# Attention stage of an audio tower on one Trainium2 core: row maxima turned on VectorE instead of TensorE, and a new order of dense products, copies, reciprocals and page clears

## The chip, the cores and the metric

The kernel runs on one core of a Trainium2 chip. The metric is the device time of one execution in microseconds, the median of several runs. The core has TensorE (PE in the rows, with PEld for its weight loads), VectorE (DVE), ScalarE (ACT), GpSimd (POOL) and SyncE (SP), whose queue issues most DMAs. Each engine works through its own list of instructions in order and waits on semaphores.

## What is computed

The input is 32 sequences of 375 tokens and 256 features. A causal mix over 32 taps with two dense layers gives `h` (376 tokens). Then come attention and a mixture-of-experts layer, each with a layer norm ahead of it and a residual behind it. Only the attention is touched by the change:

```python
q = (x @ wq + bq).reshape(b, s, h, hd).transpose(0, 2, 1, 3)      # 16 heads of 16
k = (x @ wk + bk).reshape(b, s, h, hd).transpose(0, 2, 1, 3)
v = (x @ wv + bv).reshape(b, s, h, hd).transpose(0, 2, 1, 3)
scores = jnp.einsum('bhqd,bhkd->bhqk', q, k) / jnp.sqrt(jnp.float32(hd))
scores = jnp.where(causal, scores, -jnp.inf)
weights = jax.nn.softmax(scores, axis=-1)
attn = jnp.einsum('bhqk,bhkd->bhqd', weights, v)
...
return attn @ wo + bo
```

## The kernel before

The attention phase is a software pipeline over the 32 sequences. One **step** `b` works on several sequences at once: the token mix of sequence b+3 (`mix`), layer norm, queries and keys of b+2 (`front`), the values and row maxima of b+1 (`maxima`), the exponentials of b (`attend`) and the output product of b-1 (`finish`). Steps run from -3 to 32; those from 1 to 28, twenty-eight in all, hold every part. Two steps stand in a hardware loop.

A step has 28 **units** on every engine, `n = 7*g + u` with four groups `g` (half of the heads is `g // 2`) of seven units `u`. In each unit TensorE computes scores twice: once with queries as rows for `neg_max` (L584, masked by the bf16 product of L601), which VectorE reduces to the negated row maximum (L830, function `maxima`), and once with keys as rows (L618), which ScalarE turns into exponentials (L739, `exps`). The first form has three PSUM banks, so unit n needs the maxima of unit n-3 (unit 27 and the first ones of a step have their own rule); the second has two, so unit n needs the exponentials of unit n-2. GpSimd masks the exponentials (L949) and TensorE multiplies them with the values (L654) behind units 4, 11, 18 and 25. ScalarE copies these products out (`keep`), GpSimd adds the parts of a half (`join`), VectorE shuffles the sums and takes reciprocals in four quarters (`gather_sums`: piece 0 is the shuffle L884, pieces 1 to 4 are L890), and GpSimd scales the result and splits it (`normalise`).

Between units TensorE does the **dense** products, which share two banks in turn: `hid` (n = 1, 2), `val` (7, 27), `nT` (transposes of the normed rows, L540, 9 and 10), `q` (13, 15), `k` (16, 18), `out` (21, 23), `conv` (24, 25), and `maxT` (5, 20). A product may start when the one before the last has been read. Most are read twice, since a value is carried as a high and a low float32r part: ScalarE writes the high part (`take_hi`), VectorE the low one (`take_lo`).

The maximum must be subtracted inside the exponential's product. So q_rows holds, beside three times 16 rows of queries per 64-row half of the array, two more rows, the high and low part of the negated maximum, against rows of ones in k_rows. `neg_max` has queries on partitions, so `max_T` turns it on TensorE (L566, three transposes per half), `take_hi` and `take_lo` split it (L705, L815), and four DMAs of SyncE (`max_rows`, L1088) lay it into q_rows. Half 0 is turned at unit 20 and needed at unit 0 of the next step, half 1 at unit 5 and needed at unit 14 (`open_exp` waits for max_loaded). Before a new sequence's maxima are computed these rows are set to zero by two DMAs per half (L1072).

SyncE's queue in a step, in order: the maxima of half 1 (4 DMAs), queries and keys of half 0 (`rows`, L1064: 6 each, and the 2 zero DMAs), the maxima of half 0 (4), the store of the finished rows (2, after `out1` is read), the next input (2, after `conv1` is computed), queries and keys of half 1 (14, after the step's last exponentials). That is 40 DMAs. ScalarE's queue clears two pages of DRAM of 816 KB each (L746) after units 9 and 11.

## Time and profile before

| | |
|---|---|
| time, median of 3 runs | 2151.53 us (2150.16 to 2156.01) |
| the profiled execution's own time | 2163.89 us |
| its span, first to last instruction | 2162.1 us |
| attention phase | to about 1309 us of the span |
| one full step of it | 36.95 us |
| busy in one full step | PE 35.82, DVE 30.43, ACT 22.99, POOL 19.55 us |

The routing phase and the expert pages follow the attention phase and are the same code before and after. Within a full step TensorE has almost no idle time; the number to watch is the step's length, times the count of steps.

### The profile page before, as it was taken

The page shows a single profiled execution, that of the slowest core. Times are in us where ns is not written, and L with a number is a line of the kernel's source. Part 1 is how long each engine was busy: PE and PEld are TensorE (multiplying, and loading weights), DVE is VectorE, ACT ScalarE, POOL GpSimd, SP SyncE. Part 2 cuts the span into 40 slices and gives each one's busy share as a digit, 9 for nine tenths or more (in the row PEclk, how much of TensorE's full clock was granted, in tenths as well). Part 3 has the DMA queues.
Part 4 walks back from the last instruction along what each step waited for, and adds up shares of the span by engine and source line. Part 5 has one row for each costly group of instructions (what it writes and reads, how often), then busy time and mean ns, then how long its engine had stood idle before and what let it go on. Part 6 is the DMA issues. An engine that isn't in the chain of part 4 may idle for free. (4 is left out here: it accounts for less than half of the span.)

```text
span 2162.1 us, 49812 instructions
## 1 busy us (share of the span) xinstructions
PE 1836.0 (85%) x14801; PEld 1434.1 (66%) x14802; DVE 1416.7 (66%) x3857; ACT 988.2 (46%) x2112; POOL 1054.0 (49%) x1443
## 2 busy tenths in 40 slices
PE   4899999999999999999999875877787749768674
PEld 4777777777777777777777644666666638757663
DVE  3468888888788888888887735656566542434343
ACT  1156566666566666656665543322223204323231
POOL 3035555455555555555555553445555431455555
PEclk7579999999999999999999976888888879889996
DMA  2334434434343434343433412222222246778785
GB/s 74 68 98 137 129 134 132 136 126 144 115 149 117 133 131 131 132 130 134 131 133 114 137 62 91 81 72 88 88 89 83 89 111 223 245 241 267 249 259 183
DMA packets 214515, 291.09 MB, mean 135 GB/s; under 512 B 44854, under 2 KB 176666, under 8 KB 214426
## 3 DMA queue, kind: packets, MB, share of 16 engines
q1 hardware_dynamic: 178010, 186.11, 28.2%
q0 software_dynamic: 18048, 49.31, 7.4%
q10 hardware_dynamic: 18368, 54.64, 6.6%
q8 instruction: 38, 0.62, 0.1%
q14 instruction: 51, 0.42, 0.1%
HBM read 83.25 MB, written 129.69 MB: 98 GB/s over the span
## 5 line engine op out<-in xcount | busy, mean ns | idle before, releaser
L830 DVE TENSOR_REDUCE neg_max<-bank 120x1 f32<-120x376 f32 (+2 forms) x896 | 523.6, 596 | 231.8 <-PE bank L584 228.0
L739 ACT ACTIVATE probs<-bank 128x376 f32<-128x376 f32 (+2 forms) x896 | 446.8, 520 | 270.3 <-PE bank L618 265.9
L584 PE MATMUL bank<-k_rows,q_rows 64*128 64x128 f32 (+2 forms) x1536 | 420.7, 354 | 5.4 <-DMA q_rows<-maxT_lo 4.6
L618 PE MATMUL bank<-q_rows,k_rows 64*120 64x120 f32 (+2 forms) x1536 | 382.4, 341 | 2.9 <-ACT probs L739 2.8
L949 POOL TENSOR_SCALAR_AFFINE_SELECT probs<-probs 128x512 f32<-128x512 f32 (+1 forms) x384 | 233.0, 625 | 232.3 <-ACT probs L739 232.3
L601 PE MATMUL bank<-causal,own_row 56*120 56x56 bf16 (+4 forms) x1792 | 310.5, 253 | 14.3 <-DMA k_rows<-k_flat_hi 8.2
L1815 POOL DMA_INDIRECT x_sorted<-r_normed,route x188 | 183.2, 974 | 202.2 <-DVE route L1662 149.8
L2171 POOL DMA_INDIRECT y_got<-y_sorted,p_route x188 | 182.5, 971 | 192.2 <-issue 185.2
L584 PEld LDWEIGHTS bank<-k_rows,q_rows 64*128 64x128 f32 (+1 forms) x1536 | 254.8, 192 | 8.6 <-DMA q_rows<-maxT_lo 5.5
L618 PEld LDWEIGHTS bank<-q_rows,k_rows 64*128 64x128 f32 (+1 forms) x1536 | 234.6, 186 | 8.0 <-ACT probs L739 5.1
L601 PEld LDWEIGHTS bank<-causal,own_row 64*128 64x128 bf16 (+2 forms) x1792 | 152.6, 117 | 129.6 <-issue 60.0
L654 PE MATMUL bank<-probs,val 128*32 128x376 f32 (+2 forms) x3072 | 194.3, 387 | 2.6 <-POOL probs L949 2.6
L890 DVE RECIPROCAL recip<-sums 128x94 f32<-128x94 f32 x256 | 185.1, 726 | 0.1
L654 PEld LDWEIGHTS bank<-probs,val 128*32 128x32 f32 (+1 forms) x3072 | 89.0, 112 | 98.3 <-issue 78.4
L975 POOL TENSOR_TENSOR attn_raw<-attn_raw,recip 128x376 f32<-128x376 f32 x64 | 63.6, 994 | 140.0 <-DVE recip L890 140.0
L2010 PE MATMUL pbank<-w_gate_up,xT 128*128 x816 | 114.5, 298 | 15.7 <-issue 14.9
L2010 PEld LDWEIGHTS pbank<-w_gate_up,xT 128*128 128x128 f32 x816 | 106.8, 210 | 19.6 <-issue 19.3
L2102 DVE SCALAR_TENSOR_TENSOR p_gated<-p_tanh,pbank 128x256 f32<-128x256 f32 x51 | 21.4, 420 | 145.3 <-ACT p_tanh L2064 114.5
L1500 DVE SCALAR_TENSOR_TENSOR r_tanh<-r_tanh,rbank 128x512 f32<-128x512 f32 (+1 forms) x48 | 32.2, 671 | 122.7 <-ACT r_tanh L1435 113.8
L1332 PE MATMUL rbank<-r_normedT_hi,r_up_hi 128*128 128x512 f32 (+1 forms) x96 | 49.3, 514 | 73.3 <-DVE r_hidden L1509 70.9
L1364 PE MATMUL rbank<-shared_down,r_hidden 128*128 128x256 f32 x376 | 99.1, 409 | 12.1 <-DVE base L1518 6.8
L1002 POOL TENSOR_TENSOR resid<-hid,bias_o 128x256 f32<-128x256 f32 (+1 forms) x96 | 67.6, 732 | 72.0 <-DVE out_rows L874 72.0
(226 smaller groups left out, 4294.6 us busy)
## 6 DMA issues: line engine op xcount, KB each, us to landing
x_sorted<-zeros ACTq DMA_DIRECT2D x32, 816.0 KB, 4.1
y_sorted<-zeros ACTq DMA_DIRECT2D x32, 816.0 KB, 4.3
x_rows<-x_sorted SPq DMA_DIRECT2D x51, 512.0 KB
y_sorted<-p_y_rows SPq DMA_DIRECT2D x51, 512.0 KB
q_rows<-q_flat_hi SPq DMA_DIRECT2D x256, 94.0 KB
k_rows<-k_flat_hi SPq DMA_DIRECT2D x248, 94.0 KB
q_rows<-q_flat_lo SPq DMA_DIRECT2D x128, 94.0 KB
out_dram<-base SPq DMA_DIRECT2D x47, 256.0 KB
```

What stands on the lines that cost most here:

```text
L584: last = eng.matmul(ps[0:T[t], m * w:(m + 1) * w], q[rows, slot, t * P:t * P + T[t]], k[rows, slot, 0:w], start=False, stop=(m == len(head ...
L601: eng.matmul(dst, own_row[group, h, 0:d], causal[group, h, 0:m, first:d], start=(h == 1), stop=False, skip_group_check=True)
L618: last = eng.matmul(ps[0:T[t], m * w:(m + 1) * w], k[64 * c:64 * c + 64, slot, t * P:t * P + T[t]], q[64 * c:64 * c + 64, slot, t * P:S], ...
L654: last = eng.matmul(bank_pv[32 * j:32 * j + 32, t * P:S], val[par][0:kk, t, 4 * (g // 2) + j, 32 * e:32 * e + 32], probs[g % 2][0:kk, j, O ...
L739: eng.activation(probs[g % 2][0:T[t], first:first + len(heads), OFF[t]:OFF[t] + w], bank_exp[n % 2][0:T[t], 0:len(heads) * w].rearrange("k ...
L830: eng.tensor_reduce(dst, src, AX.X, ALU.max, negate=True).then_inc(max_taken, 1)
L890: eng.reciprocal(recip[:, cols], sums[:, cols]).then_inc(recip_done, 1)
L949: eng.affine_select(out=blk, in_=blk, compare_op=ALU.is_ge, fill=0.0, base=0, pattern=[[0, 4], [1, d]], channel_multiplier=-1).then_inc(pr ...
L1364: last = eng.matmul(bank_y[t // 2][:, t % 2 * D:(t % 2 + 1) * D], hidden[c][:, t * P:(t + 1) * P], experts.down[:, c, :], start=(c == 0 an ...
L1815: eng.indirect_dma_start(x_sorted, at, normed[st.b % 4][:, t, :], None)\
L2010: last = eng.matmul(bank_gu[par][:, a * 2 * MR:(a + 1) * 2 * MR], xT[par][a // 2][:, k, a % 2 * P:(a % 2 + 1) * P], routed.gate_up[:, k, e ...
L2171: eng.indirect_dma_start(y_got[ring][:, t, k, :], None, y_sorted, at)\
```

## The change

The maxima are no longer turned on TensorE. VectorE copies the high part of `neg_max` and the low part into a tile of 32 columns per token tile, transposes all 32x32 blocks of it at once (`turn_maxima`, before unit 19 for half 0 and after unit 4 for half 1), and four DMAs lay it into q_rows, in pieces of 32 values (128 bytes). For this the four rows for the maxima of both array halves are made neighbours (rows 62 to 65), and q_rows is padded to 384 columns. The zeros take one DMA per half instead of two. A step now has 14 dense products instead of 16, and their places change: both `nT` behind unit 9, both `k` behind unit 17, `out` at 20 and 22, `conv` at 24 and 27, where `val1` follows. ScalarE keeps the value products one unit earlier (11, 18, 25), clears the pages after units 14 and 16, and makes `k` and `conv` copies at the new places. VectorE does both `hid` sums and the norm's statistics after unit 2, each low part one unit earlier where it can, and the reciprocals at other units. GpSimd joins half 0 a group earlier and adds the residual a group later.

```diff
-    ROWS = 3 * sh.HD
+    ROWS = (0, P - 3 * sh.HD)
+    MAX_ROW = P // 2 - 2
+    SPAN = NT * P
...
-        q_rows = [sb(f"q_rows{p}", [P, 8, S], F32R) for p in range(2)]
+        q_rows = [sb(f"q_rows{p}", [P, 8, SPAN], F32R) for p in range(2)]
...
-        maxT = [sb(f"maxT_{s}", [8, 2, S], F32R) for s in ("hi", "lo")]
+        max_parts = [sb(f"max_parts{h}", [P, NT, 32], F32R) for h in range(2)]
+        max_turned = [sb(f"max_turned{h}", [P, NT, 32], F32R) for h in range(2)]
...
-                return (["hid0", "hid1"] * front + ["maxT1"] * attend + ["val0"] * maxima
-                        + ["nT0", "nT1", "q0", "q1", "k0", "k1"] * front + ["maxT0"] * maxima
+                return (["hid0", "hid1"] * front + ["val0"] * maxima
+                        + ["nT0", "nT1", "q0", "q1", "k0", "k1"] * front
                         + ["out0", "out1"] * finish + ["conv0", "conv1"] * mix + ["val1"] * maxima)
...
-                def max_T(st, half, shift):
-                    ps = open_bank(st, f"maxT{half}")
-                    eng.wait_ge(max_taken, st.at(shift, GROUPS * UNITS, 2 * UNITS * (half + 1)))
-                    for t in range(NT):
-                        last = eng.transpose(ps[0:8, t * P:t * P + T[t]], neg_max[0:T[t], t, half, :],
-                                             ident[0:T[t], 0:T[t]])
-                    close(last)
...
-                        if n == 5 and st.attend:
-                            max_T(st, 1, 0)
                         if n == 7 and st.maxima:
                             values(st, 0)
-                        if n in (9, 10) and st.front:
-                            normed_T(st, n - 9)
+                        if n == 9 and st.front:
+                            normed_T(st, 0)
+                            normed_T(st, 1)
                         if n in (13, 15) and st.front:
                             query_key(st, "q", (13, 15).index(n), w_q)
-                        if n in (16, 18) and st.front:
-                            query_key(st, "k", (16, 18).index(n), w_k)
-                        if n == 20 and st.maxima:
-                            max_T(st, 0, 1)
-                        if n in (21, 23) and st.finish:
-                            out_rows_(st, (21, 23).index(n))
-                        if n in (24, 25) and st.mix:
-                            conv(st, n - 24)
+                        if n == 17 and st.front:
+                            query_key(st, "k", 0, w_k)
+                            query_key(st, "k", 1, w_k)
+                        if n in (20, 22) and st.finish:
+                            out_rows_(st, (20, 22).index(n))
+                        if n in (24, 27) and st.mix:
+                            conv(st, (24, 27).index(n))
                         if n == 27 and st.maxima:
                             values(st, 1)
...
-                        if n == 9 and st.attend:
+                        if n == 14 and st.attend:
                             clear_pages(st, x_sorted)
-                        if n == 11 and st.attend:
+                        if n == 16 and st.attend:
                             clear_pages(st, y_sorted)
-                        if n == 5 and st.attend:
-                            take_hi(st, "maxT1", maxT[0][0:8, 1, :], 8)
                         if n == 5 and st.finish:
                             keep(st, 3, -1)
                         if n == 7 and st.front:
                             normalise(st)
                         if st.front and n in (9, 10):
                             take_hi(st, f"nT{n - 9}", nT[st.b % 2][0][:, n - 9, :])
+                        if n in (11, 18) and st.attend:
+                            keep(st, (11, 18).index(n), 0)
                         if st.front and n == 13:
                             if not (isinstance(st.i, int) and st.b == -2):
                                 for h in range(2):
-                                    eng.wait_ge(rows_loaded[(st.b + 1) % 2][h], st.turn(1, 224, 224))
+                                    eng.wait_ge(rows_loaded[(st.b + 1) % 2][h], st.turn(1, 208, 208))
                         if st.front and n in (13, 15):
                             j = (13, 15).index(n)
                             take_hi(st, f"q{j}", q_flat[0][:, j, :], bias=bias_q[:, j:j + 1])
-                        if n in (12, 19, 26) and st.attend:
-                            keep(st, (12, 19, 26).index(n), 0)
-                        if st.front and n in (16, 18):
-                            j = (16, 18).index(n)
-                            take_hi(st, f"k{j}", k_flat[0][:, j, :], bias=bias_k[:, j:j + 1])
-                        if n == 20 and st.maxima:
-                            take_hi(st, "maxT0", maxT[0][0:8, 0, :], 8)
-                        if st.mix and n in (24, 25):
-                            take_hi(st, f"conv{n - 24}", mixed[0][:, n - 24, :])
+                        if st.front and n == 17:
+                            for j in range(2):
+                                take_hi(st, f"k{j}", k_flat[0][:, j, :], bias=bias_k[:, j:j + 1])
+                        if st.mix and n in (25, 27):
+                            j = (25, 27).index(n)
+                            take_hi(st, f"conv{j}", mixed[0][:, j, :])
+                        if n == 25 and st.attend:
+                            keep(st, 2, 0)
...
-                HALF_1_AT, HALF_0_AT = (10, 11, 12, 13, 16), (22, 24, 25, 26, 27)
-                HI = ["maxT1", "nT0", "nT1", "q0", "q1", "k0", "k1", "maxT0", "conv0", "conv1"]
+                HALF_1_AT = {10: (0, 1), 12: (2,), 14: (3,), 16: (4,)}
+                HALF_0_AT = {21: (0,), 23: (1, 2), 25: (3,), 26: (4,)}
+                HI = ["nT0", "nT1", "q0", "q1", "k0", "k1", "conv0", "conv1"]
...
+                def turn_maxima(st, half, shift):
+                    parts = max_parts[half][:, :, 0:16].rearrange("q t (c s m) -> q t c s m", c=2, s=2)
+                    whole = neg_max[:, :, half, :].rearrange("q t (c m) -> q t c m", c=2)
+                    done = st.at(shift, 2, half + 1)
+                    eng.wait_ge(max_taken, st.at(shift, GROUPS * UNITS, 2 * UNITS * (half + 1)))
+                    eng.tensor_copy(parts[:, :, :, 0, :], whole).then_inc(max_hi, 1)
+                    eng.wait_ge(max_hi, done)
+                    eng.tensor_tensor(parts[:, :, :, 1, :], whole, parts[:, :, :, 0, :].bitcast(F32), ALU.subtract)\
+                        .then_inc(max_lo, 1)
+                    eng.wait_ge(max_lo, done)
+                    eng.transpose(max_turned[half][:, :, :].rearrange("q t i -> q (t i)").bitcast(F32),
+                                  max_parts[half][:, :, :].rearrange("q t i -> q (t i)").bitcast(F32)).then_inc(max_turns, 1)
...
+                        if st.finish and n == 25:
+                            out_sum(st, 1)
+                        if st.mix and n == 26:
+                            take_lo(st, "conv0", mixed[1][:, 0, :], mixed[0][:, 0, :])
+                        if n == 19 and st.maxima:
+                            turn_maxima(st, 0, 1)
+                        if st.finish and n == 21:
+                            out_sum(st, 0)
                         if st.maxima:
                             maxima(st, g, u)
-                        if st.front and n in (2, 3):
-                            hid_out(st, n - 2)
-                            if n == 3:
-                                norm_stats(st)
-                        if n == 6 and st.attend:
-                            take_lo(st, "maxT1", maxT[1][0:8, 1, :], maxT[0][0:8, 1, :], 8)
+                        if st.front and n == 2:
+                            hid_out(st, 0)
+                            hid_out(st, 1)
+                            norm_stats(st)
+                        if n == 4 and st.attend:
+                            turn_maxima(st, 1, 0)
+                        if st.maxima and n == 7:
+                            values(st, 0)
+                        if st.front and n in (9, 10):
+                            j = n - 9
+                            take_lo(st, f"nT{j}", nT[st.b % 2][1][:, j, :], nT[st.b % 2][0][:, j, :])
                         if st.finish and n in HALF_1_AT:
-                            gather_sums(st, 1, -1, HALF_1_AT.index(n))
-                        if st.maxima and n in (8, 27):
-                            values(st, (8, 27).index(n))
-                        if st.front and n in (10, 11):
-                            j = n - 10
-                            take_lo(st, f"nT{j}", nT[st.b % 2][1][:, j, :], nT[st.b % 2][0][:, j, :])
-                        if st.front and n in (14, 16):
-                            j = (14, 16).index(n)
+                            for piece in HALF_1_AT[n]:
+                                gather_sums(st, 1, -1, piece)
+                        if st.front and n in (13, 15):
+                            j = (13, 15).index(n)
                             take_lo(st, f"q{j}", q_flat[1][:, j, :], q_flat[0][:, j, :], bias=bias_q[:, j:j + 1])
-                        if st.front and n in (17, 19):
-                            j = (17, 19).index(n)
-                            take_lo(st, f"k{j}", k_flat[1][:, j, :], k_flat[0][:, j, :], bias=bias_k[:, j:j + 1])
-                        if n == 21 and st.maxima:
-                            take_lo(st, "maxT0", maxT[1][0:8, 0, :], maxT[0][0:8, 0, :], 8)
+                        if st.front and n == 17:
+                            for j in range(2):
+                                take_lo(st, f"k{j}", k_flat[1][:, j, :], k_flat[0][:, j, :], bias=bias_k[:, j:j + 1])
                         if st.attend and n in HALF_0_AT:
-                            gather_sums(st, 0, 0, HALF_0_AT.index(n))
-                        if st.finish and n in (22, 23):
-                            out_sum(st, n - 22)
-                        if st.mix and n in (25, 26):
-                            j = n - 25
-                            take_lo(st, f"conv{j}", mixed[1][:, j, :], mixed[0][:, j, :])
+                            for piece in HALF_0_AT[n]:
+                                gather_sums(st, 0, 0, piece)
+                        if st.mix and n == 27:
+                            take_lo(st, "conv1", mixed[1][:, 1, :], mixed[0][:, 1, :])
+                        if st.maxima and n == 27:
+                            values(st, 1)
...
-                        if g == 2 and st.attend:
+                        if g == 1 and st.attend:
                             join(st, 0, 0)
-                        if g == 2 and st.maxima:
+                        if g == 3 and st.maxima:
                             residual(st)
...
-                        for c in range(2):
-                            at, slots = 64 * c + ROWS, slice(4 * half, 4 * half + 4)
-                            eng.dma_start(q_rows[par][at:at + 2, slots, :].bitcast(F32),
-                                          q_rows[par][at + 2:at + 4, slots, :].bitcast(F32)
-                                          ).then_inc(rows_loaded[par][half], 16)
+                        at, slots = MAX_ROW, slice(4 * half, 4 * half + 4)
+                        eng.dma_start(q_rows[par][at:at + 4, slots, 0:S].bitcast(F32),
+                                      q_rows[par][at + 4:at + 8, slots, 0:S].bitcast(F32)
+                                      ).then_inc(rows_loaded[par][half], 16)
...
-                    _, k = st.product(f"maxT{half}")
-                    eng.wait_ge(dense_read, k + 1)
-                    for c in range(2):
-                        for part in range(2):
-                            row_ = 64 * c + ROWS + part
-                            eng.dma_start(q_rows[par][row_:row_ + 1, 4 * half:4 * half + 4, :].bitcast(F32),
-                                          maxT[part][4 * c:4 * c + 4, half, :].bitcast(F32)).then_inc(max_loaded[par][half], 16)
+                    wait_alone(eng, max_turns, st.at(shift, 2, half + 1), passed_sp)
+                    rows_ = q_rows[par][MAX_ROW:MAX_ROW + 4, 4 * half:4 * half + 4, :].bitcast(F32)\
+                        .rearrange("r m (t b i) -> r m t b i", b=4, i=32)
+                    for b in range(4):
+                        eng.dma_start(rows_[:, :, :, b, :], max_turned[half][32 * b:32 * b + 16, :, :].bitcast(F32)
+                                      ).then_inc(max_loaded[par][half], 16)
```

## Rows read from the trace of the kernel before

**Rows 1.** The page: busy time, and the granted clock in 40 slices

```profile
PE 1836.0 (85%) x14801; PEld 1434.1 (66%) x14802; DVE 1416.7 (66%) x3857; ACT 988.2 (46%) x2112; POOL 1054.0 (49%) x1443
...
PE   4899999999999999999999875877787749768674
...
PEclk7579999999999999999999976888888879889996
```

**Rows 2.** Busy time by stretch: one full step

```profile
602.55:639.50 36.95, 35.82 (x352) 26.73 (x352) 30.43 (x66) 22.99 (x49) 19.55 (x29) 1.00 0.39 131
```

**Rows 3.** Waits, 200 to 1200 us: total, times, longest

```profile
PE bank L515 <- DVE out_rows L874: 14.0, 27, 0.6
PE bank L494 <- DVE normedT_lo L815: 12.8, 27, 0.5
...
PEld bank L584 <- DMA q_rows<-maxT_lo: 1.1, 1, 1.1
```

**Rows 4.** Timeline of TensorE in one step: start, duration, line

```profile
602.08 0.23 PE L601 MATMUL bank<-causal,own_row 56*120 56x56 bf16 x1
...
602.55 0.49 PE L566 MATMUL bank<-ident,neg_max 128*8 128x128 f32 x3
602.97 0.23 PE L601 MATMUL bank<-causal,own_row 56*120 56x56 bf16 x1
...
612.70 0.28 PE L601 MATMUL bank<-causal,own_row 64*128 64x256 bf16 x1
...
620.31 0.23 PE L601 MATMUL bank<-causal,own_row 56*120 56x56 bf16 x1
...
620.59 0.33 PE L618 MATMUL bank<-q_rows,k_rows 64*128 64x376 f32 x1
...
632.34 0.28 PE L601 MATMUL bank<-causal,own_row 64*128 64x256 bf16 x1
```

**Rows 5.** Timeline of VectorE in the same step

```profile
600.47 0.55 DVE L830 TENSOR_REDUCE neg_max<-bank 120x1 f32<-120x376 f32 x1
600.93 0.41 DVE L839 TENSOR_TENSOR hid<-bank,bias_mix 120x256 f32<-120x256 f32 x1
...
602.71 1.46 DVE L830 TENSOR_REDUCE neg_max<-bank 120x1 f32<-120x376 f32 x3
```

**Rows 6.** Groups by form, 200 to 1200 us: busy, mean ns

```profile
L884 DVE STREAM_SHUFFLE sums<-sums_swapped 128x376 f32<-128x376 f32 x54 | 31.7, 587 | 0.5
...
L815 DVE TENSOR_TENSOR maxT_lo<-bank,maxT_hi 8x376 fp32r<-8x376 f32 x54 | 28.7, 531 | 0.0
...
L705 ACT ACTIVATE maxT_hi<-bank 8x376 fp32r<-8x376 f32 x54 | 25.1, 465 | 0.0
```

**Rows 7.** Groups by form on VectorE behind the attention phase

```profile
L1577 DVE TENSOR_TENSOR beyond<-rbank,spare 128x16 f32<-128x16 f32 x24 | 4.1, 171 | 32.3 <-PE rbank L1378 20.8 <-issue 7.9 <-remote 3.5
...
L1537 DVE CAST top_nof<-top_no 128x8 f32<-128x8 uint32 x23 | 3.7, 163 | 0.1
```

**Rows 8.** Timeline of SyncE's queue in the same step: issue start, duration

```profile
607.73 0.63 SPq L1088 DMA_DIRECT2D q_rows<-maxT_lo  x1
617.72 1.29 SPq L1064 DMA_DIRECT2D q_rows<-q_flat_hi  x2
...
629.06 0.57 SPq L1088 DMA_DIRECT2D q_rows<-maxT_lo  x1
```

**Rows 9.** DMA issues of the whole run: count, size, us to landing

```profile
probs<-in_L_tok_bv_dram SPq DMA_DIRECT2D x2, 0.5 KB, 2.3
page_dram<-page_expert SPq DMA_DIRECT2D x2, 0.5 KB, 6.5
```

**Rows 10.** DMA packets from 606 to 613 us

```profile
DMA packets 636, 1.76 MB, mean 252 GB/s; under 512 B 64, under 2 KB 124, under 8 KB 636
```

**Rows 11.** Late attention phase: SyncE issue, TensorE wait, the clock behind it

```profile
1235.47 1.39 SPq L1088 DMA_DIRECT2D q_rows<-maxT_lo  x1
...
1239.35 0.47 PE L584 MATMUL bank<-k_rows,q_rows 64*128 64x128 f32 x1 [3.11 <-DMA q_rows<-maxT_lo]
...
1240.00:1242.00 2.00, 2.00 (x22) 1.90 (x20) 1.38 (x2) 1.15 (x2) 0.00 (x0) 0.50 0.00 0
```

16 lines of the change are left out of this document (11 added, 5 removed).

## The prediction, made before the changed kernel was run

> **What bounds the kernel now.** I read the page first. TensorE is busy in 85% of the span, and its slices stand at 9 through the first 22 of 40, which is the attention phase, with the clock granted in full from the fifth slice on [rows 1]. Then I cut one full step out by its repeating products: 36.95 us long, TensorE busy 35.82, VectorE 30.43, ScalarE 22.99 and GpSimd 19.55 [rows 2]. So within a step TensorE is the bound, and whatever shortens its list by a microsecond shortens the step by one, as long as nobody makes it wait instead. The waits confirm it and show what is left. TensorE stops at two places once per step: before q0, for the low part of `nT1`, 12.8 us in 27 steps, and before conv0, for VectorE's read of `out0`, 14.0 us in 27 [rows 3]. These are 0.47 and 0.52 us per step. DMA waits for the maxima came once in that stretch [rows 3]. The phase holds 28 full steps; the four or five ragged ones at each end wait for other things. The rest of the program is untouched.
>
> **TensorE's list.** From the timeline of one step [rows 4]:
>
> - A turn of the maxima takes from 602.55 to 602.97, 0.42 us. Two per step go: 0.84.
> - A unit with dense work behind it takes 0.47 (602.08 to 602.55), one with another unit right behind it 0.28 (620.31 to 620.59). Each interruption between units thus costs 0.19 beside its own work. There are 18 interrupted places in a step before (1, 2, 4, 5, 7, 9, 10, 11, 13, 15, 16, 18, 20, 21, 23, 24, 25, 27) and 15 after, since 5, 10 and one of 20/21 go and the other moves cancel. 3 x 0.19 = 0.57. From below I take nothing for it (the gap may come back at another seam), from above 0.57; I take 0.57, because the two spacings are of the same kind of unit.
>
> **The two stalls.** Both transposes now come behind unit 9, and VectorE takes the low parts at 9 and 10 ahead of the shuffle and the reciprocal, where they stood behind them. q0 still comes behind unit 13, so its 0.47 goes. `out0` is now multiplied behind unit 20 and read before unit 21's maximum, while before it was read behind unit 22's maximum and a shuffle; conv0 stays at 24. Its 0.52 goes too. Together 0.99.
>
> **A new stall.** VectorE does both `hid` sums and the statistics behind unit 2, so the maximum of unit 3 comes after them; before it stood between the sums. The second sum and the statistics take from 600.93 to 602.71, 1.78 us [rows 5]. They would begin at 600.47 and end at 602.25, and unit 3's maximum would end 0.46 later (1.46 for three running on), at 602.7. Unit 6 uses the same bank. Without the turn it could start at 602.08 + 0.28 = 602.36 [rows 4]. TensorE waits 0.35 there, and some 0.05 for the semaphore: 0.4. What is late next is unit 7 by 0.1 at most, then the 12 products of val0 give VectorE time to catch up. From below 0, from above 0.9 if the sum waits for its product too.
>
> **VectorE.** It loses two low parts of 0.531 us [rows 6], 1.06 per step. It gains twice a copy, a difference and a block transpose, in line, each waiting for the one before. The first two are small: 0.163 and 0.171 for shapes nearest to them [rows 7]. No transpose of blocks is in the trace. The nearest row is the shuffle within 32 partitions, 0.587 for 376 columns [rows 6]; 96 columns cannot cost more, and not less than a smallest instruction, 0.16. I take 0.25. That is 2 x 0.58 = 1.2 against 1.06. VectorE stays at 30.5 us in a step of 35, 87% busy, and the turns stand where it is ahead of TensorE by more than that (val0 behind unit 7, out0 behind unit 20). I cost them at nothing; without that cover they cost 1.2. The Trainium skill, in "VectorE: DVE Perf Modes", section "The three transpose paths", gives 311 ns for a 128x128 bf16 block transpose on VectorE, and no run shows one yet. By it VectorE's addition would be 1.3 us and the step the same.
>
> **The pairs and the other engines.** k0 and k1 in a row keep VectorE from unit 18's maximum until both low parts are done, and ScalarE from its exponential. TensorE can run three units ahead by the maxima and two by the exponentials, and behind unit 18 it has a value product, behind unit 20 `out0`. I find no wait, but such places are tight: conv1 must be read before `hid0` behind unit 1, GpSimd's residual now ends about when VectorE wants it, the join stands ahead of three masks that unit 25 needs. I bound this from 0 to 1.0 per step and take 0.3, since the present schedule shows stalls of 0.5 at just such places. ScalarE loses 2 x 0.465 [rows 6]; it is idle for a third of the step, so nothing.
>
> **The queue of SyncE.** 38 DMAs instead of 40, at some 0.65 us of issue each. For half 0 the last one was issued at 629.63 (629.06 + 0.57, rows 8) and unit 0 of the next step came at 632.34 [rows 4]: 2.7 us to land, which was enough but for one case in 27 [rows 3]. Afterwards the chain starts with q1's low part at least one maximum (0.55) earlier, has one zero DMA less (0.65), and TensorE arrives 0.42 + 0.19 + 0.52 = 1.1 earlier: 2.8 us. For half 1 the last issue ended at 608.36 [rows 8] and unit 14 came at 612.70 [rows 4], 4.3 us. It gains 0.65, TensorE comes 0.9 sooner, and the chain may start up to 1.0 later because `load_x` now waits for conv1 behind unit 27: 3.1 us. The pieces change: now 48 per DMA of 128 bytes, 192 in all. The four DMAs before were cut into pieces below 512 bytes as well, 64 packets of them in the window that holds the four [rows 10], so this is three times as many, spread over 16 engines at 40% load. I take no cost. The clears come three to five units later, off half 1's maxima and onto the first rows of the next half.
>
> **The sum.** Per full step: 0.84 + 0.57 + 0.99 - 0.4 - 0.3 = 1.70. 28 x 1.70 = 48. The eight other turns of the ragged steps give 8 x 0.6 = 5. In one ragged step TensorE stood 3.11 us for the maxima of half 1, whose issues were stretched to 1.39 us by the clears, and ran at the lower clock for some microseconds after it [rows 11]. With the clears later and one DMA less I take 2 off. In all 55 of the profiled execution's own time of 2163.89 (its span is 2162.1). Its median neighbours were 2151.53, so the forecast is 2151.53 x (1 - 55/2163.89) = 2097.
>
> **The rivals.**
>
> - **Main: as summed**, 2.3 at best and 1.2 at worst per full step: 28 x 2.3 + 10 = 74 to 28 x 1.2 + 3 = 37, that is 2078 to 2115.
> - **VectorE becomes the pace.** It had 36.95 - 30.43 = 6.5 us of waits per step [rows 2], each one for a unit not yet computed. If it can lose only a sixth of them because its new bursts (hid and statistics, two k, two reciprocals at 23) make TensorE wait in turn, the step is 30.5 + 5.4 = 35.9, a gain of 1.05, 30 us: 2122. For it speaks the busy share of 87%; against it that TensorE waits for maxima nowhere now.
> - **The maxima land late.** This is the one that ends slower. If the DMAs of 128-byte pieces need as long as the one of many tiny pieces did, 6.5 us, and not 2.3 as its neighbour [rows 9], unit 0 waits 6.5 - 2.8 = 3.7 and unit 14 waits 3.4. Per step 7.1 - 1.7 = 5.4 more, 28 x 5.4 = 151: 2302, and more if the clock falls as in rows 11. It decides from a landing time of about 3.9 us, where both waits together (3.9 - 2.8 and 3.9 - 3.1) eat 1.9. The Trainium skill, "DMA: Bandwidth & Descriptors", section "Specifications", says that below 512 bytes a transfer does not reach line rate because the engine reads, modifies and writes. It speaks against this change, and the present pieces are below that bound already.
> - **No change**: the gains are eaten by waits at the tight places, 1.7 or so per step; 2145 to 2158.
>
> **Chances.** Main 0.76, VectorE's pace 0.13, late maxima 0.06, no change 0.05. 0.3%, about 6 us, is about what a measurement of this kernel can tell from no change. Faster by more than that: 0.76 + 0.13 and the small part of late maxima that still gains, 0.90. Same 0.05, slower 0.05. The range takes in the main case and VectorE's pace with some room: 2074 to 2128.
>
> **What would show it.** After: a full step of about 35.2 us; no instruction on neg_max by TensorE; TensorE's waits before q0 and conv0 gone; a wait of about 0.4 at unit 6 for VectorE's maximum; VectorE's block transposes at 0.2 to 0.3 us; the new DMAs' issue still at 0.6 us, and no wait of scores for the turned maxima in full steps; the 3.11 wait in the ragged step about halved. The prediction is wrong if waits for `neg_max` or `probs` appear at several units of each step, if the new DMAs take clearly longer to issue or to land, or if the interruptions keep their price when there are fewer.

## The result, and the profile after

The changed kernel takes 2057.12 us (median of 4 runs, 2053.22 to 2071.27) against 2150.85 for the kernel before on the same chip (4 runs, 2143.12 to 2156.01): a ratio of 0.9587, 95% interval 0.9543 to 0.9630. The forecast was 2097 with a range from 2074 to 2128. The direction was right. The gain was 94 us where 54 were forecast, and the time is outside the range.

The page of the changed kernel, as in [rows 1]: TensorE has 67 us less to do and its share of the span stays at 85%.

```profile
PE 1768.9 (85%) x14609; PEld 1413.7 (68%) x14610; DVE 1436.8 (69%) x3985; ACT 968.6 (47%) x2048; POOL 1052.4 (51%) x1446
...
PE   4799999999999999999999848777787759667774
...
PEclk8589999999999999999999858888898879898897
```

One full step, cut at the same product as in [rows 2]; the columns are length, PE, PEld, DVE, ACT, POOL, the granted clock, the share of the DMA engines, GB/s:

```profile
589.55:623.59 34.04, 33.92 (x345) 26.23 (x346) 31.00 (x69) 22.32 (x47) 19.55 (x30) 1.00 0.57 141
```

It is 2.91 us shorter. TensorE was idle for 1.13 us of a step and now is for 0.12; the other 1.9 us is work and spacing that went, and short waits of the weight loads, which the row counts as busy. VectorE has 31.00 us of 34.04, 91%.

The measure for the comparisons below is the mean full step: the time from the start of the norm statistics in step 1 to that in step 29, divided by 28. It was 36.96 us (158.42 to 1193.23) and is 34.08 (147.83 to 1102.04). By the same landmarks the phase shrank by 98.4 us: 28 x 2.88 = 80.6 in the full steps, 10.6 ahead of them and 7.2 behind them. The program behind the phase took 5.8 us longer in the profile after (858.9 against 853.1), so that the profiled executions differ by 92.6 us. The stretch ahead of the full steps is not the change's alone: its length was 147.8, 141.6 and 152.1 us in three profiles of the same changed kernel and 136.3 to 148.2 us in ten variants of it, and it holds the time at the lower clock. The third of these profiles, at 152.1, is of an execution that was 1.5% slower than the fastest of its kernel.

The waits of TensorE from 200 to 1100 us (total, times, longest), to be held against [rows 3]:

```profile
PEld bank L602 <- DVE neg_max L829: 31.0, 129, 0.4
...
PE bank L585 <- DMA q_rows<-max_turned: 0.3, 1, 0.3
```

The waits for `normedT_lo` and `out_rows` are not in the list any more. What stands there is the weight load that waits for VectorE's maxima, in 129 short pieces. Its longest piece is in the timeline of TensorE at unit 6, which is the second row here; the third is unit 7:

```profile
592.54 0.13 PEld L602 LDWEIGHTS bank<-causal,own_row 56*120 56x120 bf16 x1 [0.19 <-issue]
...
593.20 0.13 PEld L602 LDWEIGHTS bank<-causal,own_row 56*120 56x120 bf16 x1 [0.37 <-DVE neg_max L829]
...
593.66 0.11 PEld L602 LDWEIGHTS bank<-causal,own_row 64*128 64x128 bf16 x2 [0.17 <-DVE neg_max L829]
```

VectorE in the same stretch, the turn in three instructions:

```profile
592.60 1.01 DVE L829 TENSOR_REDUCE neg_max<-bank 120x1 f32<-120x376 f32 x2
...
593.52 0.17 DVE L837 CAST max_parts<-neg_max 128x24 fp32r<-128x24 f32 x1
...
593.72 0.18 DVE L839 TENSOR_TENSOR max_parts<-neg_max,max_parts 128x24 fp32r<-128x24 f32 x1
```

And the instructions on `max_turned` in the whole run (count, shortest, median and longest ns), the DMAs' issue and the block transpose:

```profile
L1104 SPq DMA_DIRECT2D q_rows<-max_turned x256: 639/652/822, 96.2 to 1165.6; - x128
L842 DVE STREAM_TRANSPOSE max_turned<-max_parts x64: 277/278/279, 93.0 to 1163.1; 128x96 f32<-128x96 f32 x64
```

So the small prices of the forecast hold. The block transpose takes 278 ns (taken: 0.25 us), the copy and the difference 0.17 and 0.18, the issue of a DMA 0.652. The maxima land in time but for 0.3 us in one step.

### The profile page after: what moved, and what is told of

It is laid out like the page before. It is cut to its first block and busy times, and to the rows that moved or that the text cites. A ratio compares the mean times of both kernels' runs of the same rounds, so it can differ in the third digit from the quotient of the medians.

```text
span 2069.5 us, 49314 instructions
## 1 busy us (share of the span) xinstructions
PE 1768.9 (85%) x14609; PEld 1413.7 (68%) x14610; DVE 1436.8 (69%) x3985; ACT 968.6 (47%) x2048; POOL 1052.4 (51%) x1446
## 2 busy tenths in 40 slices
DMA packets 226547, 291.12 MB, mean 141 GB/s; under 512 B 57142, under 2 KB 188954, under 8 KB 226458
## 3 DMA queue, kind: packets, MB, share of 16 engines
q1 hardware_dynamic: 190042, 186.14, 36.3%
## 5 line engine op out<-in xcount | busy, mean ns | idle before, releaser
L738 ACT ACTIVATE probs<-bank 128x376 f32<-128x376 f32 (+2 forms) x896 | 440.7, 529 | 279.7 <-PE bank L619 267.9
L829 DVE TENSOR_REDUCE neg_max<-bank 120x1 f32<-120x376 f32 (+2 forms) x896 | 508.0, 587 | 60.4 <-PE bank L585 55.8
L585 PE MATMUL bank<-k_rows,q_rows 64*128 64x128 f32 (+2 forms) x1536 | 411.6, 350 | 4.0 <-ACT probs L738 2.5
L619 PE MATMUL bank<-q_rows,k_rows 64*120 64x120 f32 (+2 forms) x1536 | 373.0, 338 | 3.3 <-ACT probs L738 3.1
L602 PE MATMUL bank<-causal,own_row 56*120 56x56 bf16 (+4 forms) x1792 | 305.4, 250 | 18.3 <-DMA k_rows<-k_flat_hi 11.7
L2136 DVE COPY p_y_rows<-pbank 128x512 f32<-128x512 f32 x51 | 35.2, 689 | 90.4 <-remote 59.7
```

The source lines that it names most:

```text
L585: last = eng.matmul(ps[0:T[t], m * w:(m + 1) * w], q[rows, slot, t * P:t * P + T[t]], k[rows, slot, 0:w], start=False, stop=(m == len(head ...
L602: eng.matmul(dst, own_row[group, h, 0:d], causal[group, h, 0:m, first:d], start=(h == 1), stop=False, skip_group_check=True)
L619: last = eng.matmul(ps[0:T[t], m * w:(m + 1) * w], k[64 * c:64 * c + 64, slot, t * P:t * P + T[t]], q[64 * c:64 * c + 64, slot, t * P:S], ...
L738: eng.activation(probs[g % 2][0:T[t], first:first + len(heads), OFF[t]:OFF[t] + w], bank_exp[n % 2][0:T[t], 0:len(heads) * w].rearrange("k ...
L829: eng.tensor_reduce(dst, src, AX.X, ALU.max, negate=True).then_inc(max_taken, 1)
```

## The experiments

Ten variants ran, and the changed kernel twice more, on four chips. `e1` to `e4` ran on the first, `e5`, `e7`, `e8` and `after_again` on the second, `e9`, `e10` and `after_timed` on the third, and `e11` on the fourth. The kernel before took 2162.62, 2160.3 and 2181.02 us on the first, third and fourth. On the second it took 1993.3; the changed kernel's full step there was 34.06 us and its attention phase ended at 1207.3 us against 1210.6, so that the difference between the chips lies behind the phase. So steps are compared between chips, and times only on one. Ratios are to the kernel before on the same chip; where none is given, the kernel ran once. Diffs are against the changed kernel and are cut; the places of the copies and reads move along with them.

### The two halves of the change, each alone

`e1_turn_only`: the kernel before with the new turn; TensorE's products at their old places.

```diff
-                        if n == 9 and st.front:
-                            normed_T(st, 0)
-                            normed_T(st, 1)
+                        if n in (9, 10) and st.front:
+                            normed_T(st, n - 9)
...
-                        if n == 17 and st.front:
+                        if n in (16, 18) and st.front:
...
-                        if n in (20, 22) and st.finish:
+                        if n in (21, 23) and st.finish:
...
-                        if n in (24, 27) and st.mix:
+                        if n in (24, 25) and st.mix:
```

> The kernel before with the new way to turn alone (VectorE turns, 128-byte DMA pieces, rows 62 to 65), all other work in its old order. Theory A (each part of a full step has its own price and the prices add): two turns of 0.42 us and two interruptions of 0.19 go, the waits before q0 and conv0 stay, so a full step is 36.95 - 1.2 = 35.7 us and the run about 2151 - 28 x 1.2 - 5 = 2112 us, ratio 0.982. Theory B (VectorE's list is the pace at the tight places and the turn gains only with the new order): the added instructions of VectorE lengthen the waits for it, step 36.2 or more, ratio 0.99 or more. The share of the DMA engines rises from 0.40 to nearly 0.6 in a full step under both, since the pieces are the same as in the changed kernel.

Measured: 2158.95 us, ratio 0.9991 (0.9951 to 1.0031), full step 37.03 us. Theory A fails and theory B holds: the turn alone gives nothing. TensorE has two products less and waits instead:

```profile
PEld bank L525 <- DVE out_rows L881: 27.9, 25, 1.1
PE bank L525 <- DVE out_rows L881: 21.6, 25, 0.9
...
PE bank L504 <- DVE normedT_lo L808: 12.5, 24, 0.6
...
PE bank L602 <- DVE neg_max L823: 8.6, 24, 0.4
...
PE bank L585 <- ACT probs L736: 4.7, 25, 0.2
```

The wait ahead of conv0 grew from 0.52 to 0.86 us (21.6 in 25), the one ahead of q0 is 0.52 (0.47 before), and two come in that did not exist: 0.36 per step for the maxima, at unit 6, and 0.19 for ScalarE's exponentials, at unit 21. The DMA engines' share was expected at nearly 0.6 and is 0.45; the last section comes back to it.

`e2_order_only`: the changed kernel with the turn given back to TensorE; all else in the new order.

```diff
+                        if n == 5 and st.attend:
+                            max_T(st, 1, 0)
...
+                        if n == 20 and st.maxima:
+                            max_T(st, 0, 1)
```

> The changed kernel's order with the old way to turn (TensorE at units 5 and 20, ScalarE and VectorE parts, four row DMAs). Theory A with a cover: in the changed kernel TensorE waits 0.37 us at unit 6 for the maximum of unit 3; here a turn of 0.42 stands just there and hides that wait, so a step is 34.04 + 0.84 + 0.19 - 0.4 = 34.7 us, and the run about 2151 - 28 x 2.25 - 10 = 2078, ratio 0.966. Plain additivity instead (no cover): 34.04 + 1.22 = 35.3, ratio 0.974. The 10 us that the changed kernel gains before the first full step (its clock returns sooner) are gained here if they come from the order, and not if they come from the turn. DMA share stays at 0.40.

Measured: 2080.34 us, ratio 0.9618 (0.9583 to 0.9653), full step 34.53 us. The order alone gives 2.43 us per full step. The turn on top of it gives 34.53 - 34.08 = 0.45. The theory with a cover is near (34.7 expected), plain additivity (35.3) is not. The DMA engines' share did not stay at 0.40; it is 0.50. The stretch ahead of the full steps is 144.1 us here and 148.2 in `e1`, against 158.4 before, so it shrank with either half and decides nothing between them.

From TensorE's timelines, the stretches of a full step in us, start to start, each the mean of 27 steps ("turn" is `maxT`; all other stretches agree within 0.04 us):

```
stretch                          before   e1     e2     after
units 5 to 7, turn                2.05    2.05   2.00   1.93
units 8, 9                        1.06    0.98   1.12   0.92
nT and the units between/behind   1.90    1.97   1.59   1.60
units 12, 13                      1.35    1.41   0.81   0.80
k pair, units, value product      5.16    5.16   4.96   4.94
units 19 to 24, turn, out         6.55    6.56   5.61   5.40
conv1, unit 26/27, val1           2.66    2.66   2.47   2.47
units 0, 1                        1.48    1.50   1.25   1.25
```

### The order taken back piece by piece

`e7_nT_late`: VectorE takes the transposes' low parts one unit later, behind the shuffle.

```diff
-                HALF_1_AT = {10: (0, 1), 12: (2,), 14: (3,), 16: (4,)}
+                HALF_1_AT = {10: (0,), 11: (1,), 12: (2,), 13: (3,), 16: (4,)}
...
-                        if st.front and n in (9, 10):
+                        if st.front and n in (10, 11):
```

> The changed kernel with the low parts of nT at units 10 and 11 behind the shuffle and the reciprocal again (reciprocals at 10, 11, 12, 13, 16). My step: the wait before q0 comes back, about 0.5 us, a full step of 34.5 to 34.6. Rival: the pair of transposes already brought q0 its input in time, 34.1.

Measured: 34.70 us per full step, 1909.34 us. Against 34.06 on the same chip the step lost 0.64, 0.1 more than expected, and the wait ahead of q0 is back. In one step's timeline:

```profile
217.11 0.44 PE L504 MATMUL bank<-normedT_hi,w_q_hi 128*128 128x376 f32 x1 [0.56 <-DVE normedT_lo L814]
```

`e11_out_late`: the last product's halves back at units 21 and 23. VectorE's shuffle of half 0 moves from 21 to 22, and its read of `out0` goes behind unit 22's maximum. The expectation misnames two things: the halves stand at units 20 and 22 in the changed kernel, and the wait of 0.52 is the one ahead of conv0, not of the queries' product.

```diff
-                        if n in (20, 22) and st.finish:
-                            out_rows_(st, (20, 22).index(n))
+                        if n in (21, 23) and st.finish:
+                            out_rows_(st, (21, 23).index(n))
```

> The changed kernel with the two halves of the last product put back from units 19 and 22 to units 21 and 23, as before; the rest as changed. Theory (the early halves give the chain behind them, rescale and y_out, its time, and save 0.5 us per full step at the wait ahead of the first half of the queries' projection): the wait of about 0.52 us in front of that projection returns, and the full step is 34.6 to 34.8 us instead of 34.08. Rival (ScalarE and GpSimd now stand at other units, and the chain is in time anyway; what was saved in this stretch is only seams): 34.05 to 34.25 us. Single run, to be read by the full step: mean of the 27 full steps from sequence 1 to sequence 28.

Measured: 34.98 us per full step, 2116.09 us. Neither theory nor rival held: 0.90 us lost, more than the stall it was to bring back. The waits from 200 to 1100 us:

```profile
PEld bank L585 <- ACT probs L738: 25.7, 26, 1.0
...
PE bank L585 <- ACT probs L738: 16.8, 26, 0.7
...
PE bank L525 <- DVE out_rows L887: 4.3, 26, 0.3
```

Ahead of conv0 the product's own wait is 0.17 per step, not 0.52. The larger part is 0.65 at unit 21, where TensorE stands for ScalarE. In its timeline, two copies of a value product lie ahead of the exponential:

```profile
620.13 0.57 ACT L723 ACTIVATE sum_of_even<-bank,strip_half 128x376 f32<-128x376 f32 x1 [0.91 <-PE bank L655]
...
620.60 0.57 ACT L724 ACTIVATE attn_of_even<-bank,strip_half 128x376 f32<-128x376 f32 x1
...
621.06 0.86 ACT L738 ACTIVATE probs<-bank 128x376 f32<-128x376 f32 x2
...
621.59 0.33 PE L585 MATMUL bank<-k_rows,q_rows 64*128 64x128 f32 x1 [0.64 <-ACT probs L738]
```

In the changed kernel the same two copies start at 609.58 and 610.06 and the exponential at 610.51, the same distances; but TensorE is at `out0` from 610.24 to 611.86 and reaches unit 21 behind it. In the kernel before, the turn stood behind unit 20 and the copies behind unit 19's exponential, not ahead of it. So the early `out0` is cover for ScalarE's copies, which the new order put one unit earlier. `e11` is therefore not the old state of this stretch: with the old places of everything, `e1` needs 6.56 us for units 19 to 24, and `e11` 6.32.

`e5_keys_apart`: the key products back at units 16 and 18, with their copies.

```diff
-                        if n == 17 and st.front:
-                            query_key(st, "k", 0, w_k)
-                            query_key(st, "k", 1, w_k)
+                        if n in (16, 18) and st.front:
+                            query_key(st, "k", (16, 18).index(n), w_k)
```

> The changed kernel with k0 behind unit 16 and k1 behind unit 18 again. If the pair saves a seam (the second product follows the first at 0.17 us per matmul instead of starting anew), a full step is 34.3 us instead of 34.08. Rival: the pair's gain is small and what it costs VectorE and ScalarE in waits cancels it, 34.0 to 34.1.

Measured: 34.26 us per full step, 1893.88 us: 0.20 lost, all of it in the stretch with the key products (5.15 against 4.94). It is the price of one seam: k1 no longer follows k0.

`e8_conv1_early`: conv1 back at unit 25, its high part copied at 26.

```diff
-                        if n in (24, 27) and st.mix:
-                            conv(st, (24, 27).index(n))
+                        if n in (24, 25) and st.mix:
+                            conv(st, (24, 25).index(n))
```

> The changed kernel with conv1 behind unit 25 instead of 27 (its high part by ScalarE at 26). Theory: the wait of 0.24 us at unit 1 for the maximum of unit 27 comes back, because conv1's microsecond no longer stands between unit 27 and unit 1, a full step of 34.3. Rival: VectorE has caught up there for other reasons, 34.1.

Measured: 34.23 us per full step, 1900.66 us: 0.17 lost. The number is near the 34.3 of the theory by luck, for the wait that it names did not come back: units 0 and 1 stay at 1.23 us. conv1 by itself takes 0.96 where it took 0.79 with val1 right behind it: a seam again. VectorE's low part of conv1 stayed behind unit 27's maximum in this variant, where the kernel before has it ahead.

`after_again`: the changed kernel once more on this chip.

> The changed kernel once more, for the spread of the stretch before the first full step: it took 147.8 us in its first profile and 141.5 to 144.1 in three relatives. If that is a matter of chance in when the clock is granted, it differs here from 147.8; the full step must be 34.08 again.

Measured: 1893.01 us, 34.06 us per full step. The stretch ahead of the full steps is 141.6 us.

### Suspected costs inside the new order

`e3_hid_apart`: VectorE's two `hid` sums again behind units 2 and 3.

```diff
-                        if st.front and n == 2:
-                            hid_out(st, 0)
-                            hid_out(st, 1)
-                            norm_stats(st)
+                        if st.front and n in (2, 3):
+                            hid_out(st, n - 2)
+                            if n == 3:
+                                norm_stats(st)
```

> The changed kernel with the second hid sum and the statistics back behind unit 3's maximum. Theory A: the wait of TensorE at unit 6 (0.37 us for the maximum of unit 3) goes, a full step is 33.7 us, the run 10 us shorter than the changed kernel, ratio to the kernel before 0.954. Rival: VectorE is behind there by its whole list, the wait moves on to unit 7 and the step stays at 34.0, ratio 0.959.

Measured: 2071.63 us, ratio 0.9579 (0.9547 to 0.961), full step 34.24. As the rival said, the wait does not go: it moves from unit 6 to unit 7, where it is longer, and the step grows by 0.16 instead of staying:

```profile
PE bank L602 <- DVE neg_max L829: 9.3, 26, 0.4
```

`e4_recips_late`: half 0's shuffle and reciprocals at their old units.

```diff
-                HALF_0_AT = {21: (0,), 23: (1, 2), 25: (3,), 26: (4,)}
+                HALF_0_AT = {22: (0,), 24: (1,), 25: (2,), 26: (3,), 27: (4,)}
```

> The changed kernel with half 0's shuffle and reciprocals back at units 22, 24, 25, 26, 27. Theory A: the kernel before had a wait at unit 1 for the maximum of unit 27, because a reciprocal and other VectorE work stood behind it at the end of the step; it comes back, 0.2 to 0.3 us per step, step 34.3, ratio 0.962. Rival: VectorE has room there in the changed kernel, the step stays at 34.0.

Measured: 2074.11 us, ratio 0.9583 (0.9552 to 0.9615), full step 34.09. No change: where half 0's shuffle and reciprocals stand, among these units, doesn't matter. The wait ahead of unit 1 did not come back (units 0 and 1 take 1.26 us).

### Two tries at something better

`e9_val0_at_5`: val0 behind unit 5, so that its 12 products cover VectorE's late maxima. `e10_val0_at_5_nT_at_10`: the same, and the transposes behind unit 10.

```diff
-                        if n == 7 and st.maxima:
+                        if n == 5 and st.maxima:
                             values(st, 0)
...
-                        if n == 9 and st.front:
+                        if n == 10 and st.front:
                             normed_T(st, 0)
                             normed_T(st, 1)
```

The second part of the diff is `e10`'s alone; its copies of the transposes and half 1's reciprocals move one unit with it.

> The changed kernel with val0 behind unit 5 instead of unit 7 (VectorE reads it behind unit 6). Theory: units 5 to 7 take 1.93 us instead of the 1.45 that they take without waits, since VectorE is behind there; 1.6 us of products among them cover it. But the norm's chain (statistics, GpSimd, ScalarE) ends only just when the transposes begin now, so part of the 0.48 comes back as a wait of TensorE for the normed rows at unit 9: a full step of 33.7 to 34.0 us. Rival: VectorE's whole list is the pace, 34.1.

> As the run before, and the two transposes of normed rows behind unit 10 (ScalarE and VectorE read them at 10 and 11): the wait for the normed rows is covered too, a full step of 33.6 us, 13 us less than the changed kernel over the run. Rival: the low part of nT1 is now late for q0 and 0.3 comes back there, 33.9.

> The changed kernel on the same chip as the two others, as their yardstick: full step 34.08, ratio to the kernel before 0.957 to 0.960.

Measured on one chip: `e9` 2105.47 us, ratio 0.9738 (0.9691 to 0.9784), step 35.18; `e10` 2143.95, ratio 0.9908 (0.9874 to 0.9943), step 36.69; the changed kernel (`after_timed`) 2068.27, ratio 0.9559 (0.9523 to 0.9596), step 34.06. Both are slower than the changed kernel, outside of what theory and rival allowed (33.7 to 34.1 and 33.6 to 33.9). In `e9` TensorE comes to the transposes before their input is there, 25.4 us in 26 steps:

```profile
PEld bank L550 <- ACT normed L713: 28.1, 24, 1.2
...
PE bank L550 <- ACT normed L713: 25.4, 26, 1.1
```

The normalised rows are ScalarE's, and stand in its list behind unit 7's exponentials. With val0 ahead of units 6 and 7 they come later, while the transposes stand where they stood. In `e10`, with the transposes a unit later, that wait is gone and one for the exponentials, of the same list, is in its place:

```profile
PE bank L585 <- ACT probs L738: 25.3, 24, 1.1
```

That is 1.05 of the 2.61 us per step that `e10` loses. Most of the rest is the clock. Behind this wait, at unit 10, and shorter ones of 0.27 at units 9 and 10, the granted clock falls to 0.50, that is 1.2 GHz, for the value product behind unit 11 and unit 12:

```profile
623.88 0.42 PE L585 MATMUL bank<-k_rows,q_rows 64*120 64x376 f32 x1 [1.06 <-ACT probs L738]
...
625.52 2.71 PE L655 MATMUL bank<-probs,val 128*32 128x376 f32 x24
...
626.00:627.00 1.00, 1.00 (x12) 0.39 (x8) 1.00 (x3) 0.52 (x2) 0.00 (x0) 0.50 0.00 0
```

At the full clock this product takes 1.46 us. The clock fell so in 21 of the 28 full steps of `e10`; they last 37.1 us and the other seven 35.5. That is 21/28 x 1.57 = 1.18 us per step. In `e9`, whose wait of 0.98 is nearly as long, it fell in three steps of 28 (36.5 us against 35.0), and in the kernel before, in `e1`, in `e11` and in the changed kernel in none.

No version tried has a shorter full step than the changed kernel.

## Why the prediction was wrong, step by step

Per full step the sum was 1.70 us and the step shrank by 2.88. Split by the two halves of the change, with the forecast's own terms:

```
us per full step                   forecast                                   measured
turn alone, old order              2 x 0.42 + 2 x 0.19             = 1.22     -0.07 (e1)
order alone, turn on TensorE       2 x 0.19 + 0.99 - 0.3           = 1.07      2.43 (e2)
turn, on top of the new order      2 x 0.42 + 0.19 - 0.4           = 0.63      0.45
order, on top of the new turn      the rest of 1.70                = 0.48      2.95
```

The stall of 0.4 at unit 6 is no part of the second line, since there the turn stands in its place. What failed is above all the price of the order: 1.07 forecast, 2.43 measured. The price of the turn failed too, the other way: as an independent saving of 1.22 it does not exist. In the total the second error hid a part of the first.

**The turn ("0.84", and part of "0.57").** The forecast took the two turns off TensorE's list as a whole, with the spacing that they bring. A turn was also cover. In `e1` units 5 to 7 last 2.05 us as before, though the turn is out of them: waits took all of its place. In the changed kernel they last 1.93, since unit 6 waits 0.37 and unit 7 another 0.17 for VectorE. The prediction had the 0.4 at unit 6 as a term of its own, and that was right; for unit 7 it said 0.1 at most. It had nothing for conv0, whose wait grew by 0.34 in `e1`, and nothing for unit 21, which waits 0.19 there. In the new order the turn behind unit 20 had a dense product right behind it, and cost 0.21 in its stretch (5.61 against 5.40), not 0.42. The sentence "whatever shortens its list by a microsecond shortens the step by one, as long as nobody makes it wait instead" had the condition in it, and the sum used it only at unit 6.

**The order ("0.99", "-0.3", part of "0.57").** The parts, from the single reversals:

- The two stalls were right: both waits are gone. q0's is worth 0.64 (`e7`), 0.47 forecast.
- `out0` at unit 20 is worth 0.90 (`e11`), 0.52 forecast. Only 0.17 of it is the wait ahead of conv0; the larger part is cover for ScalarE's copies at unit 21. The forecast had the right edit and half of the mechanism.
- The seams were undercounted. The forecast's count, from 18 interrupted places to 15, is one of breaks between units. A dense product behind another dense product saves a seam of its own: 0.20 for the keys (`e5`), 0.17 for conv1 and val1 (`e8`); the transposes go from 1.90 to 1.60 in the table, where the count gave 0.19. The prediction wrote that "the other moves cancel". They don't.
- The wait at unit 1 for a maximum, about 0.23 us per step (1.48 to 1.25), was missed: in the totals it is part of the many short waits of the weight load. It went with the order (`e2` has 1.25). It is neither conv1's place on TensorE (`e8`) nor that of the reciprocals (`e4`). In the kernel before, VectorE makes conv1's low part just ahead of unit 27's maximum, which comes 0.40 us later for it; in the changed kernel, and in `e8`, it stands behind. That could be the cause, but no run tests it.

```profile
595.39 0.49 DVE L815 TENSOR_TENSOR mixed_lo<-bank,mixed_hi 128x376 fp32r<-128x376 f32 x1
595.79 0.53 DVE L830 TENSOR_REDUCE neg_max<-bank 120x1 f32<-120x376 f32 x1
...
596.38 0.11 PEld L601 LDWEIGHTS bank<-causal,own_row 64*128 64x128 bf16 x2 [0.23 <-DVE neg_max L830]
```

- The "tight places" at -0.3 did not show: `e4` moves the reciprocals at no cost, and the changed kernel has no wait for a copy or a residual in its list.

The reversals were all made with the new turn, so what they have to add up to is the 2.95 of the last line, between `e1` and the changed kernel. Each changes one stretch of the table and no other by more than 0.02. They give 0.64 + 0.90 + 0.20 + 0.17 = 1.91. The table has 0.37 for the transposes, 0.25 for units 0 and 1 and 0.18 for units 5 to 9, which no run took back by itself: 2.71. The rest is mostly in units 19 to 24, where `e11` brings back 0.92 of 1.16. The prices depend on each other: the same turn is worth -0.07 or 0.45.

**The queue.** The forecast read the 64 packets below 512 bytes in [rows 10] as pieces of the four DMAs before, and called the new pieces three times as many. In the trace these 64 are all of 4 bytes. The old DMAs moved the maxima in pieces of 1504 bytes, so the pieces of 128 were new in kind. That they cost no time was right, but not for this reason.

**The ends ("5", "2").** In all 7, measured 10.6 ahead and 7.2 behind. Behind the full steps the 3.11 us wait of [rows 11], at unit 14 of step 30, was forecast to be about halved and is gone. The same unit waits 0.44 us now, and for ScalarE:

```profile
1145.21 0.30 PE L585 MATMUL bank<-k_rows,q_rows 64*128 64x128 f32 x1 [0.44 <-ACT probs L738]
```

The only wait of TensorE for turned maxima left in these steps is 0.21 us, at unit 0 of step 30:

```profile
1130.65 0.32 PE L585 MATMUL bank<-k_rows,q_rows 64*128 64x128 f32 x1 [0.21 <-DMA q_rows<-max_turned]
```

The 10.6 ahead can't be given to the change, since that stretch differs by 10.5 us between profiles of one kernel and by 11.9 among its variants.

**The rivals.** The case that ends slower, late maxima, did not come: the DMAs of 128-byte pieces were in time. VectorE as the pace came true in part. Its busy share is 91%, and its late maxima at units 6 and 7 take back most of the turn at unit 5; but it did not stop the order's gain. The range failed because its upper gain, 2.3 per step, allowed no more than the terms that were listed; all of them at their best, 0.84 + 0.57 + 0.99 = 2.40, are still less than 2.88.

## What to carry to other kernels

A short instruction on the busiest engine may be the cover of another engine's late result: before taking its length off, look at what the next instruction waits for, and how much later than now it is ready. Price a new order by all of its seams, the ones between two products too, and check every short wait of the step's timeline, not only those that the totals rank high. When a change has two halves, forecast each alone and both together: here one gave nothing, the other nearly all, and together more than the sum. And a new wait of a microsecond in every step can cost more than its length, as in `e10`, where the clock fell behind it.

## What the hardware showed that was not expected

The four DMAs in 128-byte pieces make 12288 packets below 512 bytes more, 44854 before and 57142 after, and the queue's share of the engines went from 28.2% to 36.3% for the same 186 MB:

```profile
DMA packets 226547, 291.12 MB, mean 141 GB/s; under 512 B 57142, under 2 KB 188954, under 8 KB 226458
...
q1 hardware_dynamic: 190042, 186.14, 36.3%
```

In a window from 400 to 1000 us the share of the DMA engines was 0.40 before, 0.45 with the turn alone, 0.50 with the order alone, and 0.59 with both, at 131, 131, 142 and 144 GB/s. In engine time per full step (share x 16 engines x step) that is 237, 267, 276 and 322 us. The small pieces are not what costs it. By size, the packets of that window took:

```
mean time of a packet, ns     before   e1     e2     after
128 bytes                       -       16     -       17
1504 bytes                      76      91     98     122
```

The 384 packets of 128 bytes are 6 to 7 us of engine time per step. Nearly all of the rest of the rise is in the 1504-byte packets, of which there are about 1575 per step in all four kernels: 120 us before, then 143, 155 and 192. So each half of the change makes the same transfers take longer. That transfers which now overlap slow each other down would explain it; no run shows it. The prediction's "I take no cost" held for the time, as the engines were not full. The Trainium skill, "DMA: Bandwidth & Descriptors", section "Specifications", expects transfers below 512 bytes to fall short of line rate; the trace agrees, with 8 bytes per ns for the packets of 128 bytes against 12 to 20 for those of 1504, and in the time it cost nothing here.

The seam that [rows 4] show between a unit and dense work, 0.19 us, has the same price beside a dense product, 0.17 and 0.20 (`e8`, `e5`), and on another chip.

That the granted clock can fall in the middle of a busy phase, behind a wait of 1.06 us, is the other surprise: `e10` has it in three steps of four, and `e9`, with 0.98, in one of nine.
